# The embedding stage of a one-layer vision transformer: its chunks, merges and column sums in another order

## The reference, cut to what matters

```python
xc = concatenate((x, x_right, x_left, x_down, x_up), axis=1)
...
tokens = tokens.reshape(B, h * wgrid, p * p * C5)
normed = (tokens - mean) * rsqrt(var + 1e-5) * ln_gamma + ln_beta
h = einsum('bnd,de->bne', normed, w) + b      # 192 columns
```

## Time and profile before

| what | us |
|---|---|
| median of 3 runs | 208.26 (208.11 to 209.44) |
| the profiled execution | 207.82 |
| its span, first to last instruction | 206.1 |
| mean granted TensorE clock | 0.938 of full |
| TensorE, VectorE, ScalarE, GpSimd busy | 181.7, 134.4, 116.4, 78.4 |

### The profile page before, as it was taken

One profiled execution on the slowest core, in us unless ns is written; L12 is line 12 of the kernel. 1 busy time (PEld: TensorE's weight loads), 2 busy tenths in 40 slices (PEclk: granted clock), 3 DMA queues, 4 the chain that ended last, 5 costly groups with the idle time before them and its releaser, 6 DMA issues.

```text
span 206.1 us, 3365 instructions
## 1 busy us (share of the span) xinstructions
PE 181.7 (88%) x1124; PEld 161.3 (78%) x1124; DVE 134.4 (65%) x304; ACT 116.4 (56%) x204; POOL 78.4 (38%) x90
## 2 busy tenths in 40 slices
PE   0799996947999666689999999999999999999991
PEld 0799595937986456478989998988999899989981
DVE  4199897494549976938365574675655756756445
ACT  2287826044265230178659678687596786874610
POOL 7783004321500867602033446265344462550000
PEclk9996997996999975599999999999999999999998
DMA  6999996000180000072000260540802700000002
GB/s 128 227 339 307 238 258 144 0 0 2 12 249 10 0 0 0 5 203 64 0 3 0 84 183 0 144 123 0 240 28 72 195 2 0 0 3 0 0 0 78
DMA packets 13931, 17.21 MB, mean 83 GB/s; under 512 B 2303, under 2 KB 10112, under 8 KB 13918
## 3 DMA queue, kind: packets, MB, share of 16 engines
q1 hardware_dynamic: 13374, 17.02, 31.1%
q10 hardware_dynamic: 544, 0.03, 0.2%
HBM read 16.66 MB, written 0.39 MB: 83 GB/s over the span
## 4 chain that ended last, share of the span: by engine, by line
PE 64%; DVE 11%; SPq 9%; issue 5%; DMA 4%; POOL 3%; ACT 3%; DVEq 0%; POOLq 0%
PE ps L367 32%; PE ps L1081 17%; PE ps L1083 8%; DMA stage<-in_L_ffn_w 4%; SPq L398 2%; DVE norm L1306 2%; PE ps L953 1%; POOL rs L512 1%; PE ps L809 1%; PE ps L920 1%; DVE shifted L1151 1%; SPq L352 1%; PE ps L816 1%; SPq L355 1%; POOL raw L532 1%
## 5 line engine op out<-in xcount | busy, mean ns | idle before, releaser
L367 PE MATMUL ps<-big_r,wsplit 128*128 128x512 f32 (+1 forms) x250 | 63.4, 390 | 0.0
L1147 DVE TENSOR_TENSOR big_r<-early,big_r 128x512 fp32r<-128x512 f32 x48 | 44.2, 922 | 28.2 <-ACT big_r L328 27.4
L1081 PE MATMUL ps<-wsplit,big_r 128*128 128x384 f32 x192 | 56.8, 355 | 0.0
L367 PEld LDWEIGHTS ps<-big_r,wsplit 128*128 128x128 f32 x250 | 43.5, 192 | 6.6
L725 ACT ACTIVATE early<-ps,b1t 128x512 f32<-128x512 f32 x48 | 32.8, 683 | 27.1 <-PE ps L367 27.1
L1083 PE MATMUL ps<-wsplit,big_r 128*128 128x192 f32 x192 | 48.1, 251 | 0.0
L1083 PEld LDWEIGHTS ps<-wsplit,big_r 128*128 128x128 f32 x192 | 36.5, 190 | 1.5
L1081 PEld LDWEIGHTS ps<-wsplit,big_r 128*128 128x128 f32 x192 | 36.0, 188 | 1.9 <-issue 0.2
L328 ACT ACTIVATE big_r<-early 128x512 fp32r<-128x512 f32 x48 | 30.5, 635 | 1.5
L310 POOL TENSOR_TENSOR wsplit<-stage,wsplit 128x768 fp32r<-128x768 f32 x4 | 7.4, 1842 | 34.6 <-ACT wsplit L328 19.2
L1496 DVE SCALAR_TENSOR_TENSOR t_a<-ps,gates,merge 128x192 f32<-128x192 f32 x32 | 11.8, 411 | 12.3 <-PE ps L1083 12.3
(11 more groups left out here) (220 smaller groups left out, 271.9 us busy)
## 6 DMA issues: line engine op xcount, KB each, us to landing
stage<-in_L_ffn_w SPq DMA_DIRECT2D x4, 576.0 KB, 5.7
early<-in_L_ffn_w SPq DMA_DIRECT2D x4, 576.0 KB, 5.5
shifted<-in_L_tok_w SPq DMA_DIRECT2D x6, 288.0 KB, 9.0
early<-in_x SPq DMA_DIRECT2D x3, 512.0 KB, 6.8
stage<-in_L_ffn_w SPq DMA_DIRECT2D x4, 384.0 KB, 3.5
stage<-in_L_ffn_w SPq DMA_DIRECT2D x8, 192.0 KB, 4.5
early<-in_L_ffn_w SPq DMA_DIRECT2D x4, 384.0 KB, 3.5
early<-in_L_ffn_w SPq DMA_DIRECT2D x8, 192.0 KB, 4.4
```

The lines of the kernel that those rows point to most:

```text
L367: mm = nc.tensor.matmul(dst, lhs, rhs, start=(n == 0), stop=(n == 4))
L1081: nc.tensor.matmul(ps[:, AB[t], 0:2 * D], g_hi[:, j % NG, tok], w2c, start=(f == 0), stop=False)
L1147: return nc.vector.tensor_tensor(o, a, b, op)
```

## The change: what it does, and the diff

- TensorE transposes the six pixel groups first, then shifts gamma, then the halo groups, then the pick products.
- The half-0 gammas for the unshifted part are copied by ScalarE (`s_gb0`). `retile` of image 1 goes to VectorE. Low pixels are taken between retiles and gathers.
- VectorE merges half 0's channels 0 and 1 first, then channel 2, with the low parts (now by channel) and the halo in between; the halo chunks' weights are ready before half 1. Half 1's first step is ScalarE's (`s_scaled`); its channels are finished one by one.
- `weight_sums`, `ones_r`, `u_part` are gone. `beta_product` has two stationary columns, gamma and beta, into a bank that one product with zeros has opened; row products then give `u` and `bias` together (`u_bias`).
- Chunks go 0, 1, 2, 6, 7, 3, 4, 5, each for all four tiles. The products over squares and the small transposes stand between the halo chunks and chunk 3.
- ScalarE's `mcol` and ones copies, the splits of expert 0, and the high weights stand where the diff shows them.

```diff
@@ block.scalar
+            act.wait_ge(d_gb, 32)
+            act.wait_ge(c_ones, 1)
+            copy(gb[:, :, 0].rearrange("p h (k c) -> p h k c", c=C), gb_nat[:, :, :, 0:C]).then_inc(s_gb0, 1)
...
+            merged_high(0, 0)
+            merged_high(0, 1)
             act.wait_ge(s_hcopy, 8)
             act.wait_ge(s_hedge, 2)
             copy(xh[0:HALO, 2 * C:NX], x_halo[0:HALO]).then_inc(s_hhi, 1)
+            merged_high(0, 2)
+            act.wait_ge(s_m, 1)
+            copy(wlmh[:, 0:2 * C, D:D + 2].rearrange("p (h c) k -> p h c k", h=2),
+                 mcol[:, :, :].unsqueeze(2).broadcast_to([P, 2, C, 2])).then_inc(s_mw, 1)
+            act.wait_ge(c_ones, 3)
+            copy(wlmh[0:HALO, 2 * C:NX, D:D + 2],
+                 ones_f[0:HALO, 0:4].rearrange("p (k n) -> p k n", k=2)).then_inc(s_mw, 1)
+            act.wait_ge(d_wsh[1][0], loads_of(1, 0))
+            for c in range(C):
+                nc.scalar.activation(w_sum[:, 1, c], wsh[:, 0, 1, c * D:(c + 1) * D], ACT.Copy,
+                                     scale=gb[:, 1, 0, c:c + 1]).then_inc(s_scaled, 1)
+            act.wait_ge(s_merge, MERGES.index("halo 1") + 1)
+            copy(wlmh[0:HALO, 2 * C:NX, HIGH0:], wm_halo[0:HALO]).then_inc(s_whi, 1)
+            nc.scalar.activation(sq_halo[0:HALO], x_halo[0:HALO], ACT.Square).then_inc(s_hsq, 1)
+            act.wait_ge(d_small, 16 * SMALL_DMAS)
+            copy(wraw[:, 0:8, D:], wraw[:, 0:8, P:D]).then_inc(s_wdup, 1)
+            copy(wraw[0:E, 8, D:], wraw[0:E, 8, P:D]).then_inc(s_wdup, 1)
             act.wait_ge(s_beta, 1)
             copy(beta_part, ps[:, BETAB, 0:D]).then_inc(s_betapart, 1)
+            merged_high(1, 0)
             act.wait_ge(s_sumsq, 1)
             copy(sq_part, ps[:, SQB, :]).then_inc(s_sqpart, 1)
+            merged_high(1, 1)
+            small_high(0)
+            small_high(1)
+            merged_high(1, 2)
             act.wait_ge(s_beta, 2)
-            copy(bias_row[:], ps[:, BETAB, 0:D]).then_inc(s_bias, 1)
+            copy(u_bias[:], ps[:, BETAB, 0:2 * D].rearrange("p (k n) -> p k n", k=2)).then_inc(s_bias, 1)
             nc.scalar.activation(st4[:, 1], ps[:, BETAB, 400:400 + 2 * TT:2], ACT.Copy,
                                  scale=1.0 / FEAT).then_inc(s_meansq, 1)
-            small_high(0)
-            small_high(1)
+            small_high(2)
             act.wait_ge(d_stage[0], 16 * STAGE_DMAS)
             split_high(0, 0)
-            merged_high(1)
-            act.wait_ge(s_merge, 2 * C * SHIFTS + 2)
-            copy(wlmh[0:HALO, 2 * C:NX, HIGH0:], wm_halo[0:HALO]).then_inc(s_whi, 1)
-            small_high(2)
             split_high(0, 1)
-            act.wait_ge(s_emb, 1)
-            copy(u_part[:], ps[:, UB, 0:D]).then_inc(s_u, 1)
             small_high(3)
@@ block.gpsimd
-            pool.wait_ge(s_wlo, 3)
+            pool.wait_ge(s_wlo, 2 * C + 1)
             split_low_w1(pool, 0, 0)
@@ block.tensor, from the halo groups on
+            pe.wait_ge(s_gather, 2 * GATHERS)
+            for n in range(4):
+                k, wh = n // 2, n % 2
+                if HB_OF[n] is not None:
+                    pe.wait_ge(s_xsq, HB_OF[n] + 1)
+                    pe.wait_ge(s_xlo, HB_OF[n] + 1)
+                for w in range(4):
+                    mm = nc.tensor.transpose(ps[0:HALO, HB[n], w * P:(w + 1) * P], halo_g[:, k, 4 * wh + w, :], ident)
+                mm.then_inc(s_ht, 1)
             pe.wait_ge(c_pick, 4)
             pe.wait_ge(s_gb, 1)
...
             mm.then_inc(s_gbps, 1)
+            pe.wait_ge(s_hcopy, 6)
+            nc.tensor.matmul(ps[:, BETAB, 0:D], band[0:1, 0:P], band[0:1, 0:D], start=True, stop=False)
+            pe.wait_ge(s_gb0, 1)
+            beta_products(0)
+            pe.wait_ge(s_hcopy, 8)
+            pe.wait_ge(s_xhi, XGROUPS)
+            pe.wait_ge(s_xlo, XGROUPS)
+            pe.wait_ge(s_mw, 2)
+            for ch in ORDER[0:C]:
+                pe.wait_ge(s_wlo, ch + 1)
+                for t in range(TT):
+                    embed(ch, t)
+            beta_products(1)
+            pe.wait_ge(s_gb, 2)
             pe.wait_ge(d_halo_w, 16 * HALO_W_DMAS)
             for k in range(2):
+                beta_product(gb_halo[0:HALO, k], w_halo[0:HALO, k])
             pe.wait_ge(d_tokb, 16)
+            beta_product(band[0:1, BAND0 - 1:BAND0 + 1], tokb_row[:]).then_inc(s_beta, 1)
+            pe.wait_ge(s_wlo, C + 1)
+            pe.wait_ge(s_hhi, 1)
+            pe.wait_ge(s_hlo, 1)
+            for ch in (2 * C, 2 * C + 1):
+                for t in range(TT):
+                    embed(ch, t)
...
             mm.then_inc(s_sumsq, 1)
             pe.wait_ge(s_wdup, 2)
             small_transposes(0)
+            small_transposes(1)
+            pe.wait_ge(s_first, 1)
+            pe.wait_ge(s_betapart, 1)
+            for k in range(2):
+                nc.tensor.matmul(ps[:, BETAB, k * D:(k + 1) * D], first_rows[:, k:k + 1].broadcast_to([P, P]), beta_part,
+                                 start=True, stop=True)
+            last_chunk(0)
             pe.wait_ge(s_sqpart, 1)
...
             mm.then_inc(s_beta, 1)
+            small_transposes(2)
+            last_chunk(1)
+            last_chunk(2)
             pe.wait_ge(s_watlo, 1)
             small_transposes(3)
@@ block.vector
             dve.wait_ge(d_img[0], 16)
             retile(nc.vector.tensor_copy, 0)
+            dve.wait_ge(d_img[1], 16)
+            retile(nc.vector.tensor_copy, 1)
+            low_pixels(0)
             dve.wait_ge(d_img[2], 16)
             retile(nc.vector.tensor_copy, 2)
+            low_pixels(1)
+            dve.wait_ge(c_gath0, 1)
+            gather_halo(0)
+            gather_halo(1)
+            low_pixels(2)
+            low_pixels(3)
             dve.wait_ge(s_gbps, 1)
...
+            low_pixels(4)
+            low_pixels(5)
...
+            for s in range(SHIFTS):
+                merge(0, 0, s)
+                merge(0, 1, s)
+            merge(0, 2, 0)
+            dve.wait_ge(s_gbps, 2)
             nc.vector.tensor_copy(gb_halo[0:HALO].rearrange("p k g -> p (k g)"),
                                   ps[0:HALO, UB, 0:4]).then_inc(s_gb, 1)
+            merge(0, 2, 1)
+            low_weights(1, 0, w_sum[:, 0, 0], slice(0, P))
+            merge(0, 2, 2)
+            low_weights(2, 1, w_sum[:, 0, 1], slice(0, P))
+            merge(0, 2, 3)
+            dve.wait_ge(s_gb, 2)
+            dve.wait_ge(d_halo_w, 16 * HALO_W_DMAS)
+            merge_halo(0)
+            merge(0, 2, 4)
+            merge_halo(1)
+            dve.wait_ge(s_hhi, 1)
+            tt(xl[0:HALO, 2 * C:NX], x_halo[0:HALO], xh[0:HALO, 2 * C:NX].bitcast(F32),
+               ALU.subtract).then_inc(s_hlo, 1)
+            low_weights(3, 2, w_sum[:, 0, 2], slice(0, P))
+            low_weights(4, slice(2 * C, NX), wm_halo[0:HALO], slice(0, HALO))
+            for s in range(1, SHIFTS):
+                merge(1, 0, s)
+                merge(1, 1, s)
+            merge(1, 2, 1)
+            merge(1, 2, 2)
+            low_weights(5, C, w_sum[:, 1, 0], slice(0, P))
+            merge(1, 2, 3)
+            low_weights(6, C + 1, w_sum[:, 1, 1], slice(0, P))
+            merge(1, 2, 4)
             link(nc.vector.tensor_reduce(mask[:, 0:NK], tri_p[:], AX_X, ALU.add))
             link(nc.vector.tensor_reduce(mask[:, NK:], near[:], AX_X, ALU.min))
+            low_weights(7, C + 2, w_sum[:, 1, 2], slice(0, P))
             small_low_parts((0, 1, 2))
-            dve.wait_ge(s_emb, 1)
-            dve.wait_ge(s_u, 1)
-            tt(u_sum[:], ps[:, UB, HIGH0:LMH], u_part[:], ALU.add).then_inc(s_urow, 1)
             patch_statistics(0)
-            dve.wait_ge(s_urow, 1)
+            dve.wait_ge(s_bias, 1)
             less_mean(0)
-            dve.wait_ge(s_bias, 1)
             embedding(0)
```

More of the change, by code:

```diff
@@ L271, in vit_tower, with merged @@
         AB = [4, 5, 6, 7]
+        MERGES = [(0, c, s) for s in range(SHIFTS) for c in (0, 1)]
+        MERGES += [(0, 2, 0), (0, 2, 1), (0, 2, 2), (0, 2, 3), "halo 0", (0, 2, 4), "halo 1"]
+        MERGES += [(1, c, s) for s in range(1, SHIFTS) for c in (0, 1)]
+        MERGES += [(1, 2, s) for s in range(1, SHIFTS)]
+        def merged(half, c, s=SHIFTS - 1):
+            return MERGES.index((half, c, s)) + 1
         WGROUPS = [(0, 0, 4, 0), (1, 0, 4, 0), (0, 4, 4, 384), (1, 4, 4, 384)]
@@ L841, in small_transposes, with beta_products @@
                 mm.then_inc(s_watps, 1)
-            pe.wait_ge(s_gb, 2)
-            for half in range(2):
+            def beta_products(half):
                 for s in range(SHIFTS):
```

244 lines of the change are left out of this document (90 added, 154 removed).

## The result

The changed kernel takes 214.56 us (median of 4 runs, 212.05 to 214.62); the kernel before takes 208.19 beside it (205.85 to 209.44, 4 runs). The ratio is 1.0315, with a 95% interval of 1.0191 to 1.044: slower by some 3%, 6.4 us. I had forecast 211.0 and a range to 213.0. The direction was right; the forecast was 3.6 us too low, and the measured time lies outside the range. An identical copy, timed later, gave 214.76 and a ratio of 1.0364 [1.0287, 1.0441].

A forecast was written before the change was run, and what follows sets the result against it. The start of h at 41.02 us, end of the embedding's chain of waits, was taken to set the end. Gate +1.55, port +0.6 and clock +1.0 gave +3.15 us on 207.82, so 211.0 us; range 208.3 to 213.0.

The forecast's parts named there:

- Where it is decided: Embedding's handover: whatever moves the start of scaled embedding h from 41.02 us moves the end too.
- 1 us off 165.1: Sign of being wrong: distance from the start of h to the end differing by over 1 us from 165.1.
- When the first chunk can start: VectorE's merges begin at 16.65, not 19.11; TensorE's first chunk starts near 23.2, against 27.3 before.
- six halo gathers and two memsets 1.96: VectorE work ahead of the merges, after the third image lands, priced at 1.96 us (13.49 to 15.45 before).
- What TensorE must do from there: TensorE's queue from first chunk to second `s_beta`: 12.9 us, ending at 36.1; weight sums and 1.86 us idle go.
- The gate: ScalarE's late splits delay GpSimd's two subtractions, behind which the power for h stands: h at 42.6, +1.55 us.
- A second price: the port: VectorE's two-operand operations in `patch_statistics(0)` held by GpSimd's pair through the shared port: +0.6 us, ends 0 and 0.75.
- The clock: One half-speed TensorE stretch of 3.4 us, 1.7 us of lost work, on the path: +1.0 us, ends 0 and 1.7.
- both causes: Low clock's causes ahead of the first chunk: small products after the halo transposes, and idle from about 21.5 to 23.2.
- 1: Rival: slow small products hold VectorE's gb_halo copy and channel 2's merges, 1.3 to 2 us more, 212.3 to 213; chance 0.17.
- 2: Rival: splits start sooner than summed, the gate costs 0.65, kernel stands about still at 208.5; chance 0.15.
- 3: Rival: the shift lets the output projection run at 2.4 GHz, 2.3 us back, 207.1 or perhaps 205.6; chance 0.10.

The follow-up runs named there:

- 1: Changed kernel with ScalarE's wait for expert 0 and its two split copies moved right behind `merged_high(1, 0)`: 211.5 us.
- 6: Both moves of 5, plus GpSimd waiting for the fifth low part, not the seventh, and chunks 4 and 5 tile by tile: 208.97 us, ratio 1.0049.
- 7: Kernel before, with both splits of expert 0 moved behind `small_high(3)`: 213.75 us, ratio 1.0353.
- 2: Changed kernel with ScalarE's two small `s_mw` copies moved ahead of `merged_high(0, 0)`: 211.01 us.
- 3: Changed kernel with five unread 512-column products put into TensorE's idle stretch ahead of the first chunk: 213.21 us.
- 4: Changed kernel with beta's products over the shifted weights given 32 stationary columns instead of 2, the other 30 unread: 215.64 us.
- 8: On top of 6, chunk 3 too goes tile by tile, behind `sq_part` and `small_transposes(2)`: 209.25 us.
- 5: Also called *both early*: changed kernel with the edits of 1 and 2 together: 209.35 us, ratio 1.0092.
- 9: The changed kernel run again, unchanged: 214.76 us.
- 10: On top of 8, pick products ahead of the halo transposes and VectorE's `gb` copy ahead of `low_pixels(2)`: 211.67 us, ratio 1.0127.

## Why the prediction was right or wrong, point by point

- **Where it is decided.** Right: h moved by 6.39 of 6.8 us. In all profiles, from h to the end it is 165.1 to 167.0 us; 1 (167.0) and 6 (166.8) are more than the 1 us off 165.1 that I had named as a sign of being wrong, so the stage behind h has a spread of its own of up to 1.9 us.
- **When the first chunk can start.** The sum said 23.2, it was 24.29. Nearly all of the 1.1 is in the step "six halo gathers and two memsets 1.96": moved forward, one gather landed under GpSimd's `key_rep` (1.37) and took 1.44. The port that I priced at the statistics was not looked for at the gathers, and the kernel before had the same thing to be read. Its VectorE and GpSimd:

```profile
12.30 1.11 DVE L1169 CAST wsplit<-mcol 128x12 fp32r<-128x12 f32 x1
13.29 0.15 DVE L1172 CAST wsplit<-ones_f 112x4 fp32r<-112x4 f32 x1
```
```profile
12.08 1.31 POOL L481 TENSOR_SCALAR_AFFINE_SELECT key_rep<-key_rep 64x768 f32<-64x768 f32 x1
...
13.92 1.29 POOL L486 TENSOR_SCALAR_AFFINE_SELECT group<-group 128x16 f32<-128x16 f32 x1
15.28 0.20 POOL L488 TENSOR_SCALAR_AFFINE_SELECT group<-group 128x16 f32<-128x16 f32 x1
```

  A cast of 128x12 takes 1.11 beside `key_rep`, ending 0.02 after it, and its neighbour 0.15; and while VectorE gathers, a select over 128x16 on GpSimd takes 1.29 and the next 0.20. The gathers' 0.34 were cheap in that kernel because GpSimd was the one held.
- **What TensorE must do from there.** From the end of chunk 2 to the second `s_beta` I had 9.5 us and it was 9.9 to 10.0 (30.66 to 40.6): the second half's products 0.4 dearer, the halo chunks 0.2 and chunk 3 0.1, the row products 0.3 cheaper. The sum holds. The weight sums went, as forecast.
- **The gate.** Right. The splits went behind `u_bias`, GpSimd's pair took 3.70 (forecast 3.72), and the power stood behind it. Experiments 1 and 7 show it, one by taking it away (2.4 us of the 3.15) and one by making it alone (5.8 us). It grew because "ScalarE starts `split_high(0, 0)` at 37.15" became 41.60: the gate opens when TensorE's queue is through, and so hands on each of TensorE's delays.
- **A second price: the port.** The mechanism was right and the term too large: 0.6 forecast, 0.2 on the path (GpSimd's idle ahead of the power). VectorE's small operations were held (1.33 for two, 1.66 for one), but the holding ended with GpSimd's own pair, for which the power had to wait anyway.
- **The clock: the step that failed.** "One such stretch is 3.4 us at half speed, 1.7 us of lost work ... Ends 0 and 1.7; I take 1.0." It was 3.0 us (6.37 less 3.4) over chunks 0 to 2 alone, outside my upper end. I took the length of a stretch from the two that the kernel before had the earlier trace rows, as if it were fixed. Here TensorE had fifteen small products and then 2.47 us of idle, and the level stayed at 0.50 till about 30; with the idle gone (2) it was back at 23.6. The profiles of all ten executions with this order of chunks sort the same way. In the three with idle directly ahead of the first chunk (2.47, 1.06 and 0.81 us) chunks 0 to 2 took 6.37, 5.67 and 5.56 us; in the seven without it, 3.53 to 4.60. And I had written both causes down ahead of the sum. The Trainium skill, "TensorE: Matmul & The Clock Gate", part 1, calls the number of slow matmuls run-variable for one and the same kernel; the two executions of the changed kernel agree, with 6.37 and 5.67 for the same chunks.
- **The sum.** h was forecast for 44.2 and came at 47.41, 3.2 later: 1.1 from the first chunk, 2.0 from the clock beyond the 1.0 priced, 0.4 from TensorE's later queue, less 0.3 to 0.4 for the port. Another 0.4 came behind h.
- **The rivals.** 1 named a wait that this profile doesn't have (the gb_halo copy waited for nothing) but that appeared in 3 (0.34), 4 (1.83) and 8 (1.14). 2 fell: the splits were later than summed. 3 gave nothing in the end: 75 to 100 had a granted clock of 0.73 against 0.74. The output projection itself did take 3.65 us and not 4.56 (at 82.39, before), but the router's transposes behind it waited 2.58 us for VectorE instead of 1.71 and started 41.2 us behind h, where it was 41.0 before.

Seen backward, the loss has two parts that experiments 1 and 2 take away one at a time: the pair ahead of the power, 2.4 us, and the two small copies behind the merges, 4.1 (1.95 of start and 2.1 of clock); both together give 6.5, which is what 5 measured. The 3.15 of experiment 1 holds 0.8 of clock besides.

Open: why the executions of *both early* spread over 207.84 to 212.34, at a ratio still 0.9% above before, and what decides which instructions the lower level falls on. In 1, 4, 6, 8, 9 and 10 it took the halo transposes or the picks, with 0.68 to 1.34 us of idle ahead of them; in the profiled changed kernel, 2 and 5, with 0.51 us or less, it spared them. That is a pattern over nine executions, which no experiment was made to test. In 3 the transposes were slow with the granted clock shown at 1.00. No version here was faster than the kernel before.

## What to carry to other kernels

When work moves in an engine's queue, ask of every instruction what now stands ahead of it: here two copies of 0.2 us and one power of 0.72 us, all nearly ready, cost 6.5 us by their places. Price a low clock not by the stretches that the old order had but by what the new order puts before the big products; an idle TensorE ahead of them can cost more than the idle itself. And when VectorE's work shifts in time, look at GpSimd's timeline over its whole new place, not only where two operands make one expect it.

## What the runs showed of the hardware that was not expected

- VectorE's operations are held by GpSimd's in forms for which I had not expected it. A COPY of 128x384 took 1.44 us instead of 0.37 (changed kernel, 12.39), and a TENSOR_SCALAR over 128x2 values took 1.66 instead of 0.17 (44.66); each ended with or just after GpSimd's instruction. The Trainium skill, "SBUF — State Buffer", section "SBUF: two separate sides", names for such a lock operations in a two-port mode or with two SBUF inputs; both of these have one input, so by that page they would be in the two-port mode, which no row shows. What the rows show is that the price is what is left of GpSimd's instruction, however tiny the held one is.
- The lower clock stayed while TensorE was busy with full-sized chunks: 5.71 of the 6.50 us from 23.5 to 30.0, at 0.50. Behind small products and 2.47 us of idle, the first eleven big pairs ran at that level.
- Products of 192 moving columns take nearly the same time with 2 stationary columns and with 32. At a granted clock of 0.50 thirty instructions took 2.73 us (experiment 8) and 2.78 (experiment 4); at 1.00 the next 27 took 1.32 (changed kernel) and 1.36 (experiment 4).
